# TensorE's hardware loop in a two-layer recurrence: the loop's end moved behind layer 0's fp32 passes, the first loads in another order

## The reference

```python
def layer(x, h0, Wx, Wh, b):                 # x (8, 1024, 512), h0 (8, 512)
    xW = jnp.einsum('ntd,dh->nth', x, Wx) + b
    def step(h_prev, xw_t):
        h_next = jnp.tanh(h_prev @ Wh + xw_t)
        return (h_next, h_next)
    _, hs = jax.lax.scan(step, h0, jnp.swapaxes(xW, 0, 1))
    return jnp.swapaxes(hs, 0, 1)
x = x + layer(x, cond_1024, L0_cond_Wx, L0_cond_Wh, L0_cond_b)
x = x + layer(x, cond_1024, L1_cond_Wx, L1_cond_Wh, L1_cond_b)
```

## Time and profile before

| what | value |
|---|---|
| median of 3 runs | 2097.85 us (2097.61 to 2099.15) |
| the profiled execution | 2096.68 us |
| its span in the trace | 2094.9 us |
| TensorE busy | 2073.2 us (99%) |
| VectorE busy | 1722.8 us (82%) |
| ScalarE busy | 1122.9 us (54%) |
| mean granted TensorE clock | 0.998 |

### The profile page before, as it was taken

One profiled execution on the slowest core, in us unless ns is written; L12 is line 12 of the kernel. 1 busy time (PEld: TensorE's weight loads), 2 busy tenths in 40 slices (PEclk: granted clock), 3 DMA queues, 4 the chain that ended last, 5 costly groups with the idle time before them and its releaser, 6 DMA issues.

```text
span 2094.9 us, 213909 instructions
## 1 busy us (share of the span) xinstructions
PE 2073.2 (99%) x98468; PEld 1801.4 (86%) x98468; DVE 1722.8 (82%) x10242; ACT 1122.9 (54%) x4612; POOL 13.2 (1%) x14
## 2 busy tenths in 40 slices
PE   7999999999999999999999999999999999999998
PEld 5888888888888888888888888888888888888886
DVE  4888888888888888888888888888888888888887
ACT  2555555555555555555555555555555555555554
POOL 2000000000000000000000000000000000000000
PEclk9999999999999999999999999999999999999999
DMA  3000000000000000000000000000000000000000
GB/s 102 26 24 26 24 27 23 27 23 27 23 27 23 27 23 27 23 27 24 26 24 25 25 25 26 24 26 23 27 23 27 23 27 23 27 23 27 23 27 15
DMA packets 112495, 56.00 MB, mean 27 GB/s; under 512 B 12496, under 2 KB 111072, under 8 KB 112096
## 3 DMA queue, kind: packets, MB, share of 16 engines
q1 hardware_dynamic: 111456, 53.53, 8.9%
q10 hardware_dynamic: 864, 1.18, 0.2%
q0 software_dynamic: 32, 0.02, 0.0%
HBM read 37.90 MB, written 16.78 MB: 26 GB/s over the span
## 4 chain that ended last, share of the span: by engine, by line
PE 98%; DMA 1%; DVE 0%; issue 0%; ACT 0%; ACTq 0%; SPq 0%
PE ps_rec L236 43%; PE ps_rec L247 34%; PE ps_xw L215 21%; DMA wh<-wh_in 0%; DMA x_pe<-x_t 0%; DVE zt L398 0%; DVE z L404 0%; ACT h L325 0%; ACTq L362 0%; ACT ps_rec L320 0%; ACTq L364 0%; SPq L191 0%; SPq L179 0%; ACTq L360 0%; SPq L190 0%
## 5 line engine op out<-in xcount | busy, mean ns | idle before, releaser
L236 PE MATMUL ps_rec<-wh,h 128*32 128x128 f32 x32832 | 1260.6, 273 | 14.1 <-ACT h L325 12.2
L247 PE MATMUL ps_rec<-wh_part,h 128*32 128x128 bf16 x49056 | 1061.2, 221 | 1.7 <-issue 1.7
L325 ACT ACTIVATE h<-z 128x32 f32<-128x32 f32 x2048 | 470.3, 230 | 829.3 <-DVE z L404 812.5
L236 PEld LDWEIGHTS ps_rec<-wh,h 128*32 128x32 f32 x32832 | 829.1, 109 | 97.4 <-ACT h L325 17.9
L412 DVE TENSOR_TENSOR h<-h 128x16 f32<-128x16 f32 x4088 | 630.9, 154 | 304.3 <-ACT h L325 303.3
L247 PEld LDWEIGHTS ps_rec<-wh_part,h 128*32 128x32 bf16 x49056 | 713.3, 96 | 185.2 <-issue 2.0
L320 ACT ACTIVATE ps_rec<-ps_xw,mask 128x128 f32<-128x128 f32 x2048 | 671.5, 328 | 127.7 <-PE ps_xw L215 97.9
L398 DVE STREAM_TRANSPOSE zt<-ps_rec 128x128 f32<-128x128 f32 x2048 | 639.7, 312 | 23.1 <-PE ps_rec L247 13.1
L404 DVE TENSOR_REDUCE z<-zt 128x32 f32<-128x96 f32 x2048 | 544.9, 266 | 1.5 <-DVE zt L398 0.9
L215 PE MATMUL ps_xw<-wx,x_pe 128*32 128x128 f32 x8232 | 404.4, 273 | 0.0
L215 PE MATMUL ps_xw<-wx,x_mid 128*32 128x128 f32 x8192 | 402.0, 273 | 1.5 <-issue 1.5
(11 more groups left out here) (18 smaller groups left out, 10.4 us busy)
## 6 DMA issues: line engine op xcount, KB each, us to landing
x_pe<-x_t SPq DMA_DIRECT2D x256, 64.0 KB, 1.9
x_dve<-x_t SPq DMA_DIRECT2D x256, 64.0 KB, 2.0
out_t<-x_out SPq DMA_DIRECT2D x256, 64.0 KB, 1.5
wh<-wh_in SPq DMA_DIRECT2D x1, 1024.0 KB, 4.7
wx<-wx_in SPq DMA_DIRECT2D x1, 1024.0 KB, 8.0
wx<-wx_in ACTq DMA_DIRECT2D x2, 256.0 KB, 5.2
wx<-wx_in SPq DMA_DIRECT2D x2, 256.0 KB, 4.9
wh<-wh_in SPq DMA_DIRECT2D x2, 256.0 KB, 6.8
```

What stands on the lines that cost most here:

```text
L236: mm = pe.matmul(rows(bank, g), h_step(l, n - 1)[:, k, :], wh[l][:, k, g * P:(g + 1) * P], start=False, stop=k == KC - 1 and whole.start = ...
L247: mm = pe.matmul(rows(bank, g), h_bits(l, n - 1)[:, k, :], wh_part[l][:, i, at:at + P], start=False, stop=k == whole.start - 1 and i == PA ...
L325: act.activation(h_of(l, n), z[l][n % 2][:, :].rearrange("p (k b) -> p k b", k=KC), ACT.Tanh).then_inc(h_last if (l, n) == (0, T - 1) else ...
```

## The change

Layer 0's `recur` is cut in two. Its fp32 passes of step s + 1 (`recur_whole(0, s + 1)`) now belong to the end of slot s, and its bf16 passes (`recur_parts(0, s)`) to the beginning of slot s. In front of slot 0 stands `recur_whole(0, 0)`. The order of TensorE's matmuls stays as it was; what moves is the point at which a round ends and branches: behind layer 0's fp32 passes, in front of its bf16 passes. The last round of the loop also issues fp32 passes for a step 1024 that does not exist, into a bank that nobody reads afterwards, and so the last tanh of layer 0 counts on the common semaphore. The waits for layer 1's Wh and its parts, in front of the loop, now stand behind the fp32 passes of layer 0's step 8. The warming rounds go from (12, 6, 4) to (10, 3, 3). On SyncE's queue, `x_dve` group 1 is issued with group 0, and `x_pe` group 2 ahead of layer 1's two weight loads, behind a wait for group 0's projection.

```diff
--- before.py
+++ after.py
@@ -26,7 +26,7 @@
 RING = 8
 HALF = 4 * (P + B)
 LAG = RING
-WARM = (12, 6, 4)
+WARM = (10, 3, 3)
 IDLE = 3
 PARTED = S4
 FIRST = 1
@@ -114,7 +114,6 @@
         split_done = [[sem(f"split{l}_done{j}") for j in range(2)] for l in LAYERS]
         mid_done = sem("mid_done")
         out_done = sem("out_done")
-        h_last = sem("h_last")
         x_pe_loaded = [sem(f"x_pe_loaded{j}") for j in range(2)]
         x_dve_loaded = [sem(f"x_dve_loaded{j}") for j in range(2)]
         out_free = [sem(f"out_free{j}") for j in range(2)]
@@ -126,7 +125,7 @@
         def counted(l, s):
 
 
-            return LAG - S4 <= s < T + LAG if l else 0 <= s < T - 1
+            return LAG - S4 <= s < T + LAG if l else 0 <= s < T
 
         def h_count(l, n):
 
@@ -184,14 +183,16 @@
             for k in (0, 2):
                 sp.dma_start(wh[0][:, k, :], weights[0][1][:, k, :]).then_inc(s_wh0[k], DMA)
             sp.dma_start(x_pe[1][:, :], x[:, 1, :]).then_inc(x_first[1], DMA)
-            load(x_dve, x_dve_loaded, 0)
+            for c in range(2):
+                load(x_dve, x_dve_loaded, c)
+            sp.wait_ge(proj_done[0], 1)
+            load(x_pe, x_pe_loaded, 2)
             for e in s_wh0:
                 sp.wait_ge(e, DMA)
             sp.dma_start(wh[1][:, :, :], weights[1][1]).then_inc(s_wh1, DMA)
             sp.dma_start(wx[1][:, :, :], weights[1][0]).then_inc(s_wx1, DMA)
-            load(x_dve, x_dve_loaded, 1)
             for c in range(1, NG + 4):
-                if 2 <= c + 1 < NG:
+                if 3 <= c + 1 < NG:
                     sp.wait_ge(proj_done[0], c)
                     load(x_pe, x_pe_loaded, c + 1)
                 if c >= 4:
@@ -217,36 +218,45 @@
                 if k == KC - 1:
                     mm.then_inc(proj_done[l], 1)
 
-            def recur(l, n):
-
-
-
-
-                bank = ps_rec[l][n % 2]
-                whole = range(KC) if l == 0 and n < PARTED else range(KB[l], KC)
+            def in_parts(l, n):
+
+                return 0 if l == 0 and n < PARTED else KB[l]
+
+            def recur_whole(l, n):
+
+
                 if l or n:
                     pe.wait_ge(*h_count(l, n - 1))
                 else:
                     pe.wait_ge(s_hinit, 2)
                     pe.wait_ge(begun[0], 1)
-                for k in whole:
+                for k in range(in_parts(l, n), KC):
                     if (l, n) == (0, 0):
                         pe.wait_ge(s_wh0[k], DMA)
                     for g in range(QG):
-                        mm = pe.matmul(rows(bank, g), h_step(l, n - 1)[:, k, :], wh[l][:, k, g * P:(g + 1) * P],
-                                       start=False, stop=k == KC - 1 and whole.start == 0, skip_group_check=True,
+                        mm = pe.matmul(rows(ps_rec[l][n % 2], g), h_step(l, n - 1)[:, k, :],
+                                       wh[l][:, k, g * P:(g + 1) * P], start=False,
+                                       stop=k == KC - 1 and not in_parts(l, n), skip_group_check=True,
                                        tile_position=(0, 32 * g))
+                if not in_parts(l, n):
+                    mm.then_inc(rec_done, 1)
+
+            def recur_parts(l, n):
+
+
+                if not in_parts(l, n):
+                    return
                 if (l, n) == (0, PARTED):
                     pe.wait_ge(s_wpart[0], PARTS)
-                if is_split(l, n - 1):
-                    pe.wait_ge(*split_count(l, n - 1))
-                for k in range(whole.start):
+                pe.wait_ge(*split_count(l, n - 1))
+                for k in range(KB[l]):
                     for i in range(PARTS):
                         for g in range(QG):
                             at = k * D + g * P
-                            mm = pe.matmul(rows(bank, g), h_bits(l, n - 1)[:, k, :], wh_part[l][:, i, at:at + P],
-                                           start=False, stop=k == whole.start - 1 and i == PARTS - 1,
-                                           skip_group_check=True, tile_position=(0, 32 * g))
+                            mm = pe.matmul(rows(ps_rec[l][n % 2], g), h_bits(l, n - 1)[:, k, :],
+                                           wh_part[l][:, i, at:at + P], start=False,
+                                           stop=k == KB[l] - 1 and i == PARTS - 1, skip_group_check=True,
+                                           tile_position=(0, 32 * g))
                 mm.then_inc(rec_done, 1)
 
             def projection(s, half):
@@ -262,19 +272,29 @@
                         pe.wait_ge(mid_done, 1)
                     project(l, c, k)
 
+            def slot(s):
+
+
+
+
+                if s < T:
+                    recur_parts(0, s)
+                if s == 0:
+                    pe.wait_ge(x_first[1], DMA)
+                    project(0, 1, 0)
+                projection(s, 0)
+                if (n := number(1, s)) is not None:
+                    recur_whole(1, n)
+                    recur_parts(1, n)
+                    if T + LAG - S4 <= s < T + LAG - 1:
+                        warm(ps_rec[0][0], IDLE)
+                projection(s, 1)
+                if s < T:
+                    recur_whole(0, s + 1)
+
             def turn(r):
-
-
                 for s in range(RING * r, RING * (r + 1)):
-                    for l in LAYERS:
-                        if (n := number(l, s)) is not None:
-                            recur(l, n)
-                        if (l, s) == (0, 0):
-                            pe.wait_ge(x_first[1], DMA)
-                            project(0, 1, 0)
-                        if l and s >= T + LAG - S4 and s < T + LAG - 1:
-                            warm(ps_rec[0][0], IDLE)
-                        projection(s, l)
+                    slot(s)
 
             def warm(bank, rounds):
 
@@ -297,6 +317,7 @@
                 project(0, 0, k)
                 if k % 2:
                     warm(ps_rec[1][1], WARM[k // 2 + 1])
+            recur_whole(0, 0)
             for r in range(FIRST):
                 turn(r)
             pe.wait_ge(s_wh1, DMA)
@@ -323,7 +344,7 @@
             def tanh(l, n):
                 act.wait_ge(z_done[l], n + 1)
                 act.activation(h_of(l, n), z[l][n % 2][:, :].rearrange("p (k b) -> p k b", k=KC), ACT.Tanh).then_inc(
-                    h_last if (l, n) == (0, T - 1) else h_count(l, n)[0], 1)
+                    h_count(l, n)[0], 1)
 
             def slot(s):
 
@@ -434,7 +455,7 @@
                 if n >= 2 * S4:
                     dve.wait_ge(out_done, n - 2 * S4 + 1)
                 if n == T - 1:
-                    dve.wait_ge(h_last, 1)
+                    dve.wait_ge(*h_count(0, n))
                 add = dve.tensor_tensor(x_of(x_mid, n), x_of(x_dve, n), h_of(0, n), ALU.add)
                 if t == S4 - 1:
                     add.then_inc(mid_done, 1)
```

## The result

The changed kernel takes **2091.02 us** (median of 7 runs, 2090.55 to 2092.35) against 2097.85 (7 runs, 2096.99 to 2099.15): ratio 0.9968, 95% interval 0.9958 to 0.9978. That is 6.8 us, 0.33%, faster. In a later set it was 2089.51 against 2096.42, ratio 0.9968 again (0.9956 to 0.9980). The forecast was 2087.9, with a range from 2086.0 to 2093.4. (A ratio is taken over runs made beside each other, and so can differ from that of the medians in its last digit.)

What follows compares the result with a forecast made beforehand. TensorE, 99% busy, was taken as the bound, with 1.00 us a half slot as floor. Start 5.0 plus seam 5.0 took 10.0 us off 2096.68; with 1.17 for the median, 2087.9 us, own range 2086.3 to 2090.2, wide 2086.0 to 2093.4.

Steps and rivals of the forecast that it cites:

- bound of 2.5: At the loop's seam: the gain is only 2.5 us if each of 126 branches still costs 0.02 us.
- A: At the loop's seam: the branch stays exposed, now in front of line 247; 2092.8 us, chance 0.12.
- B: Start gives little: x wait moves to group 3, or clock is lost in slots 2 and 3; 2091.5 us, chance 0.08.
- Step 4: Loop's seam: branch fully hidden because a sequencer is held by its queue; 126 x 0.04 = 5.0 us gained.
- Step 1: Start: x group 2 loaded ahead of the 2 MB, its wait gone, slot 8 at 26.36 not 31.17; 4.8 us gained.
- Step 2: Before slot 0: fewer warming rounds, slot 0's last quarter then waiting for Wh; 0.5 us gained.
- Step 3: Slots 3 to 7: instructions asked for sooner while the 2 MB are moving; 0.3 us lost.
- Step 5: The rest: step 1024's passes fall into idle time, layer 1 waits cost zero, first round's 5.5 us stalls unchanged.
- C: At the loop's branch: the sequencer reaches it only when the array has drained; slower, 2122 us, chance 0.04.
- D: In the loop: the round is no longer held, instructions fetched anew each round; 2780 us, chance 0.01.

Runs made afterwards that it cites:

- turn_only: The changed kernel with the loads and warming rounds of before, so only the loop is turned: 2092.42 us, ratio 0.9976 to the kernel before.
- half_turn: The changed kernel with its loop ended in the middle of layer 0's fp32 passes, 8 records before the branch and 8 after: 2105.02 us, ratio 1.0041.
- no_pool_reads: The changed kernel with GpSimd filling the bf16 parts of layer 1's Wh with zeros instead of making them from Wh: 2086.47 us, ratio 0.9948.
- old_warming: The changed kernel with the warming rounds of before (12, 6, 4): 2089.44 us, ratio 0.9966 to the kernel before.
- parted_6: The changed kernel with layer 0's bf16 passes beginning at step 6 instead of 4: 2087.57 us, ratio 0.9950; in another set 2087.22, ratio 0.9953.
- parted_6_split_b: The changed kernel with bf16 passes from step 6 and layer 1's Wh loaded in two halves, second run: 2087.18 us, ratio 0.9951.
- loads_only: The kernel before with only the change's loads and warming rounds, its loop as it was: 2095.35 us, ratio 0.9989.

## Why the prediction was right, and where it was not

**The total was right in its wide range and not in its reasons.** 2091.02 lies outside the forecast's own range, 2086.3 to 2090.2 (whose upper end, by its bound of 2.5, should read 2090.4). It lies in the wide range only because that was stretched to take in rivals A and B, and what happened was neither of them. That part is luck.

**Step 4, the seam: right in sign and size** (5.0 predicted, 5.0 by the runs of `turn_only`, 4.9 by the profiles). Its reason for taking "loss 0", that a sequencer is held by its queue, was wrong here, and that the loss came out as 0 all the same is luck as well. The branch is hidden, but not because the queue is long: 16 fp32 records are work enough, 0.44 us, with the 0.06 from first load to first pass, to cover the 0.18 us that the branch comes after the first load, its own 0.21 and the 0.06 to the next load (0.45 together, against 1013.17 - 1012.68 = 0.49, by this one seam). The margin is 0.04 us (over all seams of that trace 0.02 at the least and 0.06 in the median), and `half_turn` shows what is left when the work is half as long. The rounds came out at 16.02 and 16.01 us in the median of the changed kernel's two profiles, from 16.05, not always at the 16.00 to 16.01 of the prediction; why some executions have longer ones is open.

**Step 1, x group 2: the wait went, the gain did not all come.** Predicted 4.8 us to slot 8, with steps 2 and 3 5.0; measured 1.8. The step that failed is the sentence that GpSimd's parts of layer 1's Wh "are wanted only in slot 8" and so cost nothing. They were priced by who waits for their result, and not by what they hold while they are made. The trace of before had the sign of it, in two adds of VectorE ahead of the idle stretch that took 1.02 us in place of 0.18, and I had not looked at them. The second, and the GpSimd instruction with which it ends (16.95 and 16.90):

```profile
15.93 1.02 DVE L438 TENSOR_TENSOR x_mid<-x_dve,h 128x32 f32<-128x32 f32 x1
```

```profile
15.01 1.89 POOL L388 TENSOR_TENSOR wh_rest<-wh 128x1024 f32<-128x1024 f32 x1 [0.19 <-DMA wh<-wh_in]
```

When layer 0's Wh lands differs between executions, so the term is best measured from slot 1 to slot 8: 19.1 us before (12.11 to 31.17), 14.2 in `no_pool_reads` (11.45 to 25.62), 17.5 and 17.8 in the two profiles of the changed kernel (from 11.88 and 11.51). The term of 4.8 itself was right (4.9), and 3.3 to 3.7 us of it were given back to a new wait and to the half clock that came with it.

**Step 2** (0.5 us) was too large already in front of that wait, and cannot be seen behind it. Not the last quarter but the last half of slot 0 waited for Wh: 16 records, 10.24 to 10.88, so slot 0 ends 0.2 us earlier than at 11.10, and slot 1 starts 0.2 earlier (11.88, not 12.11). **Step 3** (0.3 us lost to instruction transfers) did not happen: no such stall stands between slot 3 and slot 8 in `no_pool_reads`. **Step 5** holds: the passes of step 1024 fall into idle time (from the last round's last projection passes to slot 1024's fp32 passes it is 1.16 us, 2070.59 to 2071.75, as before, 2075.89 to 2077.05), and the first round has its five stalls and its 21.7 us.

**Rivals.** A (the seam only moves) and C (the branch waits for the passes) are out, but C's idea, a sequencer held up, is true of waits. B came true in its outcome, a start that gives little (forecast for B 2091.5, measured 2091.02), but by another mechanism than either it named. x group 3 was not waited for (slot 5 comes on the beat in `no_pool_reads`). The clock of the changed kernel fell at 20.7 and 22.3 us in its two profiles, in or behind the new idle time, and in `old_warming` at 20.1, in the same wait; without that wait (`no_pool_reads`, `parted_6`) it did not fall. B's own clock loss, in slots 2 and 3, did occur in two executions of neighbouring kernels (`parted_6_split_b`, `half_turn`); whether the fewer warming rounds have a part in that is open. D did not occur: from 51.1 us to the end four instruction transfers come in. The forecast's total was off by 3.1 us, and by the two halves the start accounts for it: 2.1 us in `loads_only` where 5.0 were predicted, 5.0 in `turn_only` where 5.0 were.

## What to carry to other kernels

Before a wait is removed, list every engine that worked during it, and what it holds while it works: that work will now run beside something, and here GpSimd's reads ran at the cost of VectorE's two-input instructions (2.89 us in place of 0.38). A hardware loop's end belongs behind long work whose own wait is released early, and in front of work that is released late; what has to fit into that work is the branch, its start after the last wait, and the first load behind it, some 0.45 us here.

## What the runs showed that was not expected

- A VectorE subtraction of 0.18 us took 1.03 and another 1.82, each ending some 0.03 us behind a GpSimd instruction that read SBUF; beside GpSimd memsets, 5.4 us of them in place of 5.7 of reading work, both kept their time.
- A compare-and-branch takes 0.208 us on TensorE's sequencer, and in these traces starts only behind the last semaphore wait that held the sequencer: 0.12 us after the first load released by it with 8 records behind the wait, 0.18 with 16, 0.32 with 32. Moving a loop's end by 8 matmul records cost 0.11 us a round.
- The array's 126 rounds differ between executions of one kernel by up to 2.4 us (`parted_6` and `parted_6_b`, 2020.1 and 2017.7), and the stretch from slot 8 to the first branch, with the stalls, by 1.4 (21.8 and 20.4 in the changed kernel). So one profile of each kernel tells a seam of 0.04 us a round only roughly.
- TensorE's clock was half from about 16.2 us on in two of nine profiles with the new loads and the fewer warming rounds, behind gaps of 0.85 and 1.00 us that the other seven have too.
